# First scores among the last value units, output products one head per step, and a context tile used in two orders

## The reference, cut to what matters

```
x = x + einsum('bct,bcd->bdt', x, weights[subjects])        # a small mixing layer
q, k, v = x @ Wq.T, x @ Wk.T, x @ Wv.T                      # 32, 8 and 8 heads of 128
q, k = rope(rmsnorm(q) * wq), rope(rmsnorm(k) * wk)
k_all, v_all = concat(pages of the cache (512 keys), new k, new v)   # 544 keys per sequence
scores = q . k_all / sqrt(128), masked by the sequence's length
o = softmax(scores) @ v_all
x = x + o.reshape(.., 4096) @ Wo.T
```

## Time and profile before

| | us |
|---|---|
| three runs, median | 1056.09 |
| their range | 1053.84 to 1056.35 |
| the profiled execution | 1053.23 |
| its span, first to last instruction | 1051.4 |
| TensorE matmuls busy | 1002.2 (95%) |
| VectorE busy | 775.6 (74%) |
| ScalarE busy | 708.5 (67%) |
| GpSimd busy | 519.7 (49%) |

### The profile page before, as it was taken

How to read it: one execution, slowest core, us unless ns; L and a number is a source line. 1 busy time by engine, 2 the same in 40 slices (tenths; PEclk the granted TensorE clock), 3 DMA queues, 4 the chain that set the end, 5 groups by cost and what they waited for, 6 DMA issues and landing times.

```text
span 1051.4 us, 25156 instructions
## 1 busy us (share of the span) xinstructions
PE 1002.2 (95%) x8585; PEld 806.7 (77%) x8585; DVE 775.6 (74%) x1641; ACT 708.5 (67%) x1959; POOL 519.7 (49%) x642
## 2 busy tenths in 40 slices
PE   4899999999889899999999999999999999999998
PEld 2578888887678688779868968977977886896893
DVE  7789999999997788648737846855864873784680
ACT  5898999988765788647737836745754773683670
POOL 6445666567881356526525534633542652563440
PEclk9999999999999999999999999999999999999999
DMA  6789999989989899749957974983984995697440
GB/s 203 251 280 342 323 386 362 392 282 400 366 283 353 330 347 297 243 133 315 306 165 226 344 224 154 326 274 107 344 262 128 306 311 168 217 349 228 146 157 11
DMA packets 200432, 279.72 MB, mean 266 GB/s; under 512 B 26481, under 2 KB 158065, under 8 KB 197745
## 3 DMA queue, kind: packets, MB, share of 16 engines
q1 hardware_dynamic: 181616, 210.86, 59.8%
q0 software_dynamic: 18688, 67.25, 18.7%
HBM read 231.77 MB, written 46.27 MB: 264 GB/s over the span
## 4 chain that ended last, share of the span: by engine, by line
PE 60%; DVE 13%; DMA 10%; ACT 6%; issue 5%; POOL 3%; SPq 3%; ACTq 0%; DVEq 0%; POOLq 0%
PE ps_o L1320 16%; PE ps_proj L1320 13%; PE ps_o L1445 10%; PE ps_t L1420 6%; DMA vs<-v_pages,v_row 6%; PE ps_s L1409 5%; PE ps_s L1413 5%; PE ps_rt L1375 2%; DMA w_nat<-in_L_cond_Wq 2%; DVE rot L1149 2%; DVE c_stage L1177 2%; DVE probs L1256 2%; POOL probs L807 1%; PE ps_o L1459 1%; SPq L594 1%
## 5 line engine op out<-in xcount | busy, mean ns | idle before, releaser
L807 POOL TENSOR_SCALAR probs<-probs,recip 128x544 f32<-128x544 f32 x256 | 184.1, 719 | 329.6 <-DVE recip L1264 324.2
L1256 DVE CUSTOM_DVE_ANT_0 probs<-ps_s,mask,row_scale 128x544 f32<-128x544 f32 x256 | 200.0, 781 | 163.5 <-PE ps_s L1413 158.1
L944 ACT ACTIVATE probs<-probs,neg_max 128x544 f32<-128x544 f32 x256 | 191.6, 748 | 141.4 <-DVE neg_max L1256 119.3
L1445 PE MATMUL ps_o<-pt_hi,vs 128*128 128x128 f16 x2048 | 213.0, 219 | 4.3 <-DMA vs<-v_pages,v_row 4.2
L951 ACT ACTIVATE pt_hi<-ps_t 128x512 f16<-128x512 f32 x256 | 149.4, 584 | 76.3 <-PE ps_t L1420 74.8
L1445 PE MATMUL ps_o<-pt_lo,vs 128*128 128x128 f16 x1024 | 184.6, 219 | 0.0
L761 POOL TENSOR_TENSOR roped<-rot 128x256 f32<-128x256 f32 x160 | 143.8, 920 | 82.1 <-DVE rot L1141 72.5
L1268 DVE SCALAR_TENSOR_TENSOR pt_lo<-ps_t,pt_hi 128x512 f16<-128x512 f32 x256 | 174.3, 681 | 5.1 <-ACT pt_hi L951 2.2
L1445 PEld LDWEIGHTS ps_o<-pt_hi,vs 128*128 128x128 f16 x2048 | 167.8, 98 | 10.2 <-DMA vs<-v_pages,v_row 6.1
L1320 PE MATMUL ps_proj<-wt_hi,x0t_hi 128*128 128x512 f32 x384 | 159.0, 414 | 8.0 <-DVE x0t_lo L1037 7.0
L793 POOL DMA_INDIRECT vs<-v_pages,v_row x128 | 130.8, 1022 | 56.5 <-PE ps_proj L1320 33.9
(11 more groups left out here) (145 smaller groups left out, 1608.3 us busy)
## 6 DMA issues: line engine op xcount, KB each, us to landing
kt<-k_pages_t SPq DMA_DIRECT2D x512, 128.0 KB
c_nat<-in_L_cond_k_cache SPq DMA_DIRECT2D x32, 512.0 KB, 6.0
q_t<-stage SPq DMA_DIRECT2D x64, 256.0 KB, 6.7
c_nat<-in_L_cond_v_cache SPq DMA_DIRECT2D x32, 512.0 KB, 6.8
qt<-q_t SPq DMA_DIRECT2D x32, 512.0 KB
w_nat<-in_L_cond_Wq SPq DMA_DIRECT2D x8, 1024.0 KB, 7.3
k_pages_t<-c_stage SPq DMA_DIRECT2D x16, 512.0 KB, 5.6
c_nat<-in_L_cond_Wo SPq DMA_DIRECT2D x16, 512.0 KB, 7.5
```

Of the source, the lines that this page charges most:

```text
L807: pool.tensor_scalar(probs_of(i), probs_of(i), col(recip, i), 1.0, ALU.mult, ALU.mult).then_inc(p_norm, 1)
L944: act.activation(pr, pr, ACT.Exp, bias=col(neg_max, i), scale=-1.0, accum_out=col(row_sum, i)).then_inc(a_exp, 1)
L1256: dve.tensor_tensor_reduce(out=probs_of(i), in0=ps_s[:, score_cols(i):score_cols(i) + KEYS], in1=mask[(i // HK) % 2][:, mask_at(i):mask_at ...
L1445: ins = pe.matmul(ps_o[n % 2][:, jl * P:(jl + 1) * P], v[:, part, :], p[i % NPT][:, c, :], start=jl == 0 and c == 0 and k == 0, stop=False ...
```

## The change

- **First scores.** The scores, maxima and exponentials of steps 0, 1 and 2 are issued in units 93, 94 and 95 (`SCORES_AT = NU - 3`), each behind its unit's products, where they followed the last unit. Tiles are placed anew in memory so that nothing early is overwritten.
- **Output products.** `y_heads` gives one head to nearly each of the steps from the last of a group (number 31) to number 28 of the next; steps 3 and 4 take two, steps 29 and 30 none. For the last group the heads follow in four blocks of 4, 6, 6 and 16. They are summed in a bank of their own, `ps_y`, over all 32 heads, and the residual is added once a group.
- **Banks.** For `ps_y` the transpositions have two banks (`NTB = 2`).
- **The context tile in two orders.** Groups with an odd number store token by token with the 32 heads side by side, those with an even number in another order with 8 heads side by side, so that each quarter of one order is what one sequence of the other overwrites. Weights are read from it with a step of 32 or 8 elements; the rows of x0 and of the output are moved in a matching order.
- **Wo and values.** 12 heads of Wo are converted early and 20 late; its loads are spread otherwise (units 84, 86, 88, 91, the rest with later keys). GpSimd loads the values of the second sequence in steps 0 to 3, behind the normalisations.

```diff
+    ps_y = psum("ps_y", [P, HID])
-    NTB = 3
+    NTB = 2
-    WO_LOADS = {84: 0, 85: 1, 87: 2, 89: 3, 92: 4}
-    WO_EARLY, WO_EARLY_AT = 16, 87
+    WO_LOADS = {84: 0, 86: 1, 88: 2, 91: 3}
+    WO_WITH_KEYS = {1: (5,), 2: (6,), 3: (7,)}
+    WO_EARLY, WO_EARLY_AT = 12, 87
+    SCORES_AT = NU - 3
-    STEPS = NP2 + 2 * HPC + 3
+    STEPS = NP2 + HPC
+    Y_AT = {r: (r + 1,) for r in range(-1, 3)} | {3: (4, 5), 4: (6, 7)} | {r: (r + 3,) for r in range(5, HQ - 3)}
+    Y_LAST = {-1: range(0, 4), 0: range(4, 10), 1: range(10, 16), 2: range(16, HQ)}
+    Y_OUT, Y_OUT_LAST = HQ - 3, 3
...
+    def head_tokens(tile, g, n):
+        if g % 2 == 1:
+            return tile[:].rearrange("p (m h) -> p m h", h=HQ)[:, :, n]
+        k, j = divmod(n, QUARTER)
+        return tile[:].rearrange("p (k m j) -> p k m j", k=GB, j=QUARTER)[:, k, :, j]
...
     def ot_of(tile, n):
         b, h = divmod(n, NHALF)
-        hh = HQ // NHALF
-        return tile[:, hh * h:hh * (h + 1), b % GB, :]
+        g, a = divmod(b, GB)
+        if g % 2 == 1:
+            return tile[:].rearrange("p (a t s h) -> p a s t h", a=GB, t=SEQ, s=NHALF)[:, a, h]
+        return tile[:].rearrange("p (s q a j) -> p s q a j", s=NHALF, a=GB, j=QUARTER)[:, h, :, a]
...
             def store_out(g):
-                sp.wait_ge(v_res, NHALF * (g + 1))
-                sp.dma_start(out[GB * g:GB * (g + 1)].rearrange("b s t -> (b s) t"), result[g % 2][:]
+                sp.wait_ge(v_res, g + 1)
+                sp.dma_start(row_order(out[GB * g:GB * (g + 1)].rearrange("b s t -> (b s) t"), g), result[g % 2][:]
...
+                if i == 0:
+                    pool.wait_ge(t_proj, NU)
+                if i < NCH:
+                    load_v(1, i)
...
+                if u == NU - 1:
+                    masked_max(u - SCORES_AT)
+                    row_recip(u - SCORES_AT - 1)
                 dve.wait_ge(a_proj, u + 1)
...
+            def project_out(g, n):
+                h = head_at(g, n)
+                if g == 0:
+                    wo_done(pe, h + 1)
+                if n == 0:
+                    if g >= 1:
+                        pe.wait_ge(v_res, g)
+                    pe.wait_ge(v_otlo, NBG * (g + 1) - 1)
+                if n == HQ // NHALF:
+                    pe.wait_ge(v_otlo, NBG * (g + 1))
+                hi, lo = head_tokens(ot_hi, g, n), head_tokens(ot_lo, g, n)
+                ins = products(ps_y[:], [(hi, wo[:, h, 0, :]), (hi, wo[:, h, 1, :]), (lo, wo[:, h, 0, :])],
+                               first=n == 0, last=n == HQ - 1)
+                if n % QUARTER == QUARTER - 1:
+                    ins.then_inc(t_y, 1)
...
                 products(ps_proj[u % NPJ][:], pairs).then_inc(t_proj, 1)
+                if u == SCORES_AT:
+                    pe.wait_ge(v_scale, 3)
+                    pe.wait_ge(v_wsum, HK)
+                if u >= SCORES_AT:
+                    scores(u - SCORES_AT)
...
-                if y_part(i) is not None:
-                    project_out(*y_part(i))
+                for n in y_heads(i):
+                    project_out(y_group(i), n)
```

More of the change, by code:

```diff
@@ L155, in build @@
     wt_hi, wt_lo = [], []
+    NSQ = 4
+    squares = []
     for i in range(2):
@@ L190, in build @@
     ps_rt = [psum(f"ps_rt{i}", [P, CH]) for i in range(2)]
+    ps_proj = [psum(f"ps_proj{i}", [P, CH]) for i in range(NPJ)]
     phase1.close()
@@ L703, in _ @@
             sp.wait_ge(d_x0, 16)
-            for k in range(len(WO_LOADS), HQ // WO_LOAD):
-                load_wo(k)
+            load_wo(len(WO_LOADS))
             for b in range(B):
@@ L710, in _ @@
                     load_new_v(b + 1)
-                g, rest = divmod(b - 2, GB)
-                if rest == 0:
+                for k in WO_WITH_KEYS.get(b, ()):
+                    load_wo(k)
+                g, rest = divmod(b - GB - 1, GB)
+                if rest == 0 and g >= 0:
                     if g >= 1:
@@ L1069, in wo_low, with add_residual @@
+            def add_residual(g):
+                dve.wait_ge(t_y, GB * (g + 1))
+                dve.wait_ge(d_res[g % 2], 16 * (g // 2 + 1))
+                dve.scalar_tensor_tensor(result[g % 2][:], ps_y[:], y_unscale[:, 0:1], result[g % 2][:],
+                                         ALU.mult, ALU.add).then_inc(v_res, 1)
             def wo_low(n):
@@ L1284, in add_residual @@
-            def add_residual(w):
-                g, half = divmod(w, NHALF)
-                dve.wait_ge(t_y, w + 1)
-                if w >= 1:
-                    dve.wait_ge(v_res, w)
-                if half == 0:
-                    dve.wait_ge(d_res[g % 2], 16 * (g // 2 + 1))
-                dve.scalar_tensor_tensor(result[g % 2][:], ps_y(w)[:], y_unscale[:, 0:1], result[g % 2][:],
-                                         ALU.mult, ALU.add).then_inc(v_res, 1)
-            for i in range(AHEAD):
-                masked_max(i)
-                if i >= 1:
-                    row_recip(i - 1)
@@ L1300, in _ @@
                     add_residual(y_out(i))
-                if at(i, OE) is not None and y_part(i) is not None:
-                    ot_lo_of(at(i, OE))
                 if i + AHEAD < NP2:
@@ L1306, in _ @@
                     row_recip(i + AHEAD - 1)
-                if at(i, OE) is not None and y_part(i) is None:
+                if at(i, OE) is not None:
                     ot_lo_of(at(i, OE))
@@ L1478, in _ @@
-            for i in range(AHEAD):
-                scores(i)
+                    wo_done(pe, h + 1)
+                if n == 0:
+                    if g >= 1:
+                        pe.wait_ge(v_res, g)
[5 more added lines that the diff above has]
+                               first=n == 0, last=n == HQ - 1)
```

323 lines of the change are left out of this document (161 added, 162 removed).

## The result

The changed kernel takes 1136.5 us (1135.21 to 1137.86) beside 1054.96 us for the kernel before (1051.99 to 1056.35): a ratio of 1.0777, 95% interval 1.0750 to 1.0803, or 81.5 us more. The prediction was 1138, with 82.6 us more.

The account below looks back on a forecast made before the run. TensorE was taken as the bound. Hand-over -2, first steps +19.1, later steps +65.5 and end 0 gave +82.6 us on the profiled 1053.23, so 1135.8, or 1138 us in terms of the runs' median; range 1104 to 1181.

Parts of the forecast that it names:

- hand-over, T(0): From the projections' last product to the first attention transposition: between 4.9 us gained and 2 lost, taken as -2 us.
- steps 0 to 32: First attention steps, no output products yet: eight rounds of 11.30 us less 3 make 87.4 us, +19.1.
- round with products: Four successive attention steps with a head of output products each: 7.90 + 2.60 + 1.45 = 11.95 us.
- steps 32 to 252: Attention steps with output products: 55 rounds of 11.95 us, less 1.2, make 656.1 us against 590.6, +65.5.
- the end, from T(252): Last steps to the final product: 29.9 us against 30.1, final sum and store unchanged, taken as 0.
- The three stalls: Three of a round's five transposition jobs wait for VectorE's low halves: 0.48, 0.34 and 0.63 us, 1.45 together with products.
- TensorE's idle time ahead of transpositions: Sign expected in the profile after: waits for VectorE's low halves, about 100 us, at exactly three of five jobs.
- the bank does not bind: Rival: low halves end before TensorE needs the bank, so the change is faster, some 1046 us; chance 0.07.
- only TN's wait binds: Rival: only the transpositions of the values' probabilities wait, 0.63 to 1.28 us a round, about 1090 us; chance 0.06.
- Strides: Strided context tile, its writing and weight loads: nothing taken; upper end 43 us if the low half doubles.
- the rival with dear strided operands: Rival: strided context access is costly, 43 us on top of the stalls, 1181 us; chance 0.12.
- The most that a reordering can win: TensorE's idle time in the groups: at most 1.15 us a group against 85.15 now, seven groups giving 8 us.

Follow-up runs that it names:

- the kernel that never waits: Changed kernel with VectorE's transposition low halves ahead of the maximum in every step and ScalarE's exponentials one step later: 1042.64 us, ratio 0.9885; again 1042.13 us.

## Why the prediction was right

By its own steps, in the profiled executions:

| step | predicted | measured |
|---|---|---|
| hand-over, T(0) | 357, gain 2 | 358.33, gain 0.85 |
| steps 0 to 32 | 87.4 (+19.1) | 446.45 - 358.33 = 88.12 (+19.9) |
| round with products | 11.95 | 11.94 |
| steady group | near 95 | 95.29 |
| steps 32 to 252 | 656.1 (+65.5) | 1102.27 - 446.45 = 655.82 (+65.2) |
| the end, from T(252) | 0 | 1135.8 - 1102.27 = 33.53, before 1051.4 - 1018.04 = 33.36 (+0.2) |
| span | +82.6 | +84.4 |

- **The three stalls.** With the step lengths of the kernel that never waits as the measure, TN starts 0.54 us late (706.36 against 705.38 + 0.44), T(4k) 0.50 (709.10 against 706.36 + 2.68 - 0.44) and T(4k+1) 0.37 (2.83 against 2.46): 1.41 of the 1.44 by which the round is longer, beside 0.63, 0.48 and 0.34, together 1.45, of the prediction. The sum is nearer than its terms: one was somewhat large, two somewhat small. TN's was given too much: its low half ended at M + 2.05 as counted (704.25 to 706.30), but the release took 0.06 us, there and at the other 63 TN, and not 0.14. What carried the prediction was to time each release from the maximum, not from VectorE's idle time. Of its signs one came out lower: TensorE's idle time ahead of transpositions adds up to 70.0 us on the list of waits, where about 100 was named; by start times, beside the kernel without stalls, it is 93.5 (655.82 against 578.66 and 88.12 against 71.82).
- **That all three bind, and separately.** The runs with one release moved show it: each took away its own stall in the groups, and the others stayed. That of T(4k+1) was moved only with the other two; its step then takes 2.46 us instead of 2.83. The rival "the bank does not bind" is excluded, and the rival "only TN's wait binds" too.
- **Steps 0 to 32.** Right within 0.7 us, with the longer stalls of steps without a head.
- **Hand-over.** A gain of 0.85 where 2 was taken. That the Wo load would stand in the way was right: in the eight kernels with the early scores T(0) comes 10.30 to 10.32 us after ScalarE's first row behind that load, wherever this row stands.

```profile
348.02 1.33 ACT L937 ACTIVATE wo<-wo,scale 128x512 f16<-128x512 f32 x2 [4.18 <-DMA wo<-in_L_cond_Wo]
```

  It starts at 348.02 where it was 345.64, 2.4 us later, beside an estimate of 2.6. That they agree is luck: the row stands between 344.92 and 350.13 in those eight, and between 344.24 and 346.93 in the five with the loads of before. T(0) stands at 355.23 to 360.45 in the eight and at 358.08 to 361.15 in the five, so a term of this size lies within what executions differ by.
- **Strides.** "I take nothing" was right, and the rival with dear strided operands falls by the run with the strides alone. Of its two parts, the low half did not change; the weight load did, to less than the 0.188 that the upper bound had allowed, and stayed hidden. That run has the step of 32 alone; with both orders, in the changed kernel, the low half takes 672 ns and the loads 143 to 147.
- **The most that a reordering can win** was priced too low: 7 x 1.15 + 2, some 1046 us. With the stalls gone the time is 1042. The 85.15 us of a group that the 1.15 came from stands in no row: from T to T the six whole groups of the kernel before take 84.9 to 86.4, so steps 32 to 252 had 12 us to give and not 8. Waits for pages, which the prediction did not look for, are a part of that.

By the rule of the Trainium skill's SBUF — State Buffer, section "Door 1: The DMA port swizzle", a step of 32 halves pays at each access; the trace agrees for the weight loads, which take that step, 144 ns against 98. The Trainium skill's TensorE: Matmul & The Clock Gate, section "Weight-path perf modes", lets weight loads take such steps; the trace has them longer but without effect. The prediction let that first rule move the sum towards its upper end, where the low half doubles. But the low half does not write single halves with that step; it writes runs of 16 or 8, and took 677 ns against 678.

## What to carry to other kernels

When a rotation of buffers is cut by one, list for each job of a round who releases its buffer, at which place of which engine's queue, and behind what; the idle share of that engine tells nothing. A release should stand ahead of work that waits for the waiting engine. But follow the moved instruction round all queues: here the right order on one engine closed a loop over another, and only both orders changed together, with the change, gave a kernel faster than the first.

## What the runs showed of the hardware

A 128-column f16 weight load from a tile read with a step of 32 (or 8) elements takes 143 to 147 ns instead of 98; in a stream of 512-column matmuls 0.216 us apart it showed nothing (ratio 1.0003, 0.9983 to 1.0024, for the step of 32 alone). VectorE and ScalarE read 512 f32 elements of a PSUM partition with a step of 32 and write them as f16 in runs of 16 in the time of contiguous ones (677 ns against 678, and 580 against 582 for the high half). From the end of a low half on VectorE to the start of the transposition that waits for it passed 0.14 to 0.15 us at the T of the changed kernel, and 0.06 at its 64 TN; why these differ is not known. The rows of the changed kernel in the group of 95.29 us (its L1356 holds the products, here with the step of 8):

```profile
L1356 PEld LDWEIGHTS ps_y<-wo,ot_hi 128*128 128x128 f16 x64 | 6.8, 147 | 0.3
...
L1141 DVE SCALAR_TENSOR_TENSOR ot_lo<-ps_o,ot_hi 128x512 f16<-128x512 f32 x8 | 5.4, 672 | 0.0
...
L930 ACT ACTIVATE ot_hi<-ps_o 128x512 f16<-128x512 f32 x8 | 4.6, 576 | 0.0
...
L1356 PEld LDWEIGHTS ps_y<-wo,ot_lo 128*128 128x128 f16 x32 | 4.6, 143 | 2.4
```
